# Second cross-attention stream of a decoder layer: VectorE takes all maxima of a unit before its copies and scalings

## The reference, cut to what matters

```python
q = (query @ Wq.T + bq)   # 16 heads of 32; k and v from the context
QEr = jnp.einsum('bhsd,ld->bhsl', q, Er)
Srel = _skew(QEr)
QK = jnp.einsum('bhsd,bhtd->bhst', q, k)
attn = (QK + Srel) / math.sqrt(dh)
attn = jnp.where(causal[None, None], attn, -jnp.inf)
attn = jax.nn.softmax(attn, axis=-1)
out = jnp.einsum('bhst,bhtd->bhsd', attn, v)
x = _layernorm(x + out)
```

## Time and profile before

| | |
|---|---|
| median of 3 runs | 4609.83 us (4608.87 to 4615.19) |
| the profiled execution | 4609.45 us, of which 4607.6 us are the span |
| PE busy | 3910.4 us (85%) |
| DVE busy | 2465.7 us (54%) |
| ACT busy | 1573.2 us (34%) |
| POOL busy | 902.6 us (20%) |
| maxima L785 | 512 instructions, 373.3 us |
| transposes L1127 | 2304 matmuls, 321.9 us |
| mean granted TensorE clock | 0.952 |

### The profile page before, as it was taken

The page is one execution under the profiler, slowest core; times in us unless marked ns, Lnnn a source line. Parts: engine busy times, 40 slices in busy tenths (PEclk is TensorE's granted clock), DMA queues, the critical chain, the costliest instruction groups (busy, mean ns, idle before and its releaser), DMA issues. The chain is left out here.

```text
span 4607.6 us, 89417 instructions
## 1 busy us (share of the span) xinstructions
PE 3910.4 (85%) x36730; PEld 2369.2 (51%) x36730; DVE 2465.7 (54%) x4665; ACT 1573.2 (34%) x3005; POOL 902.6 (20%) x1012
## 2 busy tenths in 40 slices
PE   6999897889998878799988787999887837999992
PEld 3666444546664445466644454666444523444441
DVE  3666335766664357666643576767335763222224
ACT  2444125744441257344412573444125710000000
POOL 2333100113331001133310011333100101222220
PEclk8999899999999999999999999999999978999996
DMA  7332258633322586332225863322258613544545
GB/s 245 102 88 83 83 194 305 202 102 102 90 82 83 198 303 202 104 102 86 82 83 205 299 203 107 95 86 81 83 205 301 205 67 91 125 114 125 127 116 167
DMA packets 257093, 659.34 MB, mean 143 GB/s; under 512 B 20752, under 2 KB 70080, under 8 KB 253456
## 3 DMA queue, kind: packets, MB, share of 16 engines
q1 hardware_dynamic: 241264, 616.06, 40.2%
q0 software_dynamic: 15120, 35.46, 4.0%
q10 hardware_dynamic: 320, 2.23, 0.1%
HBM read 384.84 MB, written 210.11 MB: 129 GB/s over the span
## 5 line engine op out<-in xcount | busy, mean ns | idle before, releaser
L481 ACT ACTIVATE sc<-sc,nmax 128x1024 f32<-128x1024 f32 x512 | 587.3, 1147 | 904.0 <-DVE nmax L679 903.2
L445 POOL TENSOR_SCALAR sc<-sc,pinv 128x1024 f32<-128x1024 f32 x512 | 572.5, 1118 | 1357.3 <-DVE pinv L687 1340.5
L951 PE MATMUL psum<-pts,wct 32*64 32x256 f32 x8192 | 470.3, 380 | 69.8 <-PEq L946 64.5
L679 DVE CUSTOM_DVE_ANT_0 sc<-psum,table_a 128x1024 f32<-128x1024 f32 x256 | 313.2, 1224 | 346.7 <-PE psum L935 252.4
L951 PE MATMUL psum<-xall,wct 32*64 32x256 f32 x8192 | 473.4, 380 | 19.2 <-issue 19.1
L785 DVE CUSTOM_DVE_ANT_0 sc<-psum,big 128x896 f32<-128x896 f32 (+7 forms) x512 | 373.3, 748 | 216.2 <-PE psum L1113 177.7
L925 PE MATMUL psum<-xt,w_all 128*128 128x256 f32 x1792 | 419.2, 387 | 15.0 <-PEq L920 15.0
L481 ACT ACTIVATE sc<-sc,xmax 128x896 f32<-128x896 f32 (+7 forms) x512 | 394.5, 772 | 70.1 <-DVE xmax L785 64.7
L951 PEld LDWEIGHTS psum<-pts,wct 32*64 32x64 f32 x8192 | 331.5, 133 | 157.3 <-issue 121.3
L925 PEld LDWEIGHTS psum<-xt,w_all 128*128 128x128 f32 x1792 | 333.0, 191 | 141.1 <-issue 99.9
L455 POOL TENSOR_SCALAR_AFFINE_SELECT big<-big 128x256 f32<-128x256 f32 (+1 forms) x192 | 92.6, 482 | 1325.2 <-DMA big<-skew_d 1325.1
(11 more groups left out here) (160 smaller groups left out, 5634.1 us busy)
## 6 DMA issues: line engine op xcount, KB each, us to landing
wct<-xall SPq DMA_DIRECT2D x576, 128.0 KB, 2.4
big<-skew_d SPq DMA_DIRECT2D x48, 1024.0 KB, 5.2
w_sb<-w_dram SPq DMA_DIRECT2D x48, 1024.0 KB, 5.4
big<-skew_d SPq DMA_DIRECT2D x48, 768.0 KB, 4.4
table_a<-rows_d SPq DMA_DIRECT2D x33, 960.0 KB, 5.6
table_b<-rows_d SPq DMA_DIRECT2D x33, 960.0 KB, 7.7
big<-skew_d SPq DMA_DIRECT2D x32, 896.0 KB, 4.6
big<-skew_d SPq DMA_DIRECT2D x32, 640.0 KB, 4.7
```

Of the source, the lines that this page charges most:

```text
L445: pool.tensor_scalar(sc[k % 4][:, :], sc[k % 4][:, :], pinv[:, k % 4:k % 4 + 1], 1.0, ALU.mult, ALU.mult).then_inc(probs_scaled, 1)
L481: act.activation(tile, tile, ACT.Exp, bias=least, scale=-1.0, accum_out=total).then_inc(probs_ready, 1)
L679: dve.tensor_tensor_reduce(sc[k % 4][:, :], SLOT[h], table[h][:, off:off + S], -1.0, BIG, ALU.add, ALU.min, nmax[:, k % 4:k % 4 + 1]).then ...
L951: mm = pe.matmul(OSUM[HEAD[h], a, :], v_all[rows, ST * (b % GROUPS) + b // GROUPS, HEAD[h]], ptf[h][rows, QG * b:QG * b + QG], start=(b == ...
```

## The change

On VectorE, in the loop of the second stream, the maxima of all heads of unit u are taken before the two parts. The parts keep the copies, the reciprocal and the scaling, in the order they had. No other engine's code is changed, and no wait, buffer or instruction is added or removed.

```diff
@@ -821,11 +821,10 @@
                     for t in range(ST):
                         if LAST[XV - ST + t] + 7 == u:
                             row_stats(t)
+                    if u < NU:
+                        for i in range(len(UNITS[u][2])):
+                            add_relative(u, i)
                     for part in range(2):
-                        if u < NU:
-                            nh = len(UNITS[u][2]) // 2
-                            for i in range(nh * part, nh * part + nh):
-                                add_relative(u, i)
                         if 1 <= u < NU + 1:
                             half = -(-TURNS[u - 1] // 2)
                             for g in (range(half), range(half, TURNS[u - 1]))[part]:
```

## The result

Over 20 runs of each the changed kernel takes 4600.25 us (median, 4590.91 to 4611.43) against 4613.45 us before (4604.31 to 4627.61). The ratio is 0.9973, with a 95% interval from 0.9965 to 0.9981: 12.5 us, 0.27% faster. The forecast was 4591.5 us, 18 us faster, with a range from 4576 to 4608. In the profiled execution the span is 4599.9 us.

The account below looks back on a forecast made before the run. TensorE's scores waited for VectorE's maxima (134.6 us), its weighing for the scaling (67.8 us). Per batch -2.14 - 3 x 0.85 + 0.2 = -4.5 us, four batches -18: 4591.5 us, range 4576 to 4608.

Parts of the forecast that it names:

- The gain: Iterations making scores of the first halves (two heads) of tiles 5 to 7: next scores 0.88 us sooner each, 2.64 together.
- No gain: Iterations of the second halves of tiles 5 to 7: full or nearly full of TensorE work; only 0.05 us gained, in 5b.
- Iterations 0 and 1: Iterations of tiles 0 and 1: what 0 gives, 1 takes back waiting for the last exponential; nothing for the two.
- The cost: Iterations of tiles 2, 3 and both halves of 4: weighing waits for the scaling, now behind all maxima; 1.84 us lost.
- The sum: A steady quad, twelve iterations: -2.64 - 0.05 + 1.84 = -0.85 us, from 48.07 to 47.2.
- first quad: First twelve units of a batch, starting behind a mask: 2.14 us shorter.
- last quad: Last quad of a batch, row statistics ahead of maxima in 5b to 7a: 0 to 0.6 us lost, 0.2 taken.
- The clock: Rival, iterations 2 to 4a: TensorE idles before weighings and its clock halves; 3 us per steady quad, 4628 us; 11%.
- The exponentials: Rival, 5b, 6b, 7b: transposes wait for ScalarE's second exponential, 0.3 us in hand; 12 us back, 4603 us; 14%.
- The scaling hidden: Rival, iterations 2 to 4b: weighing doesn't stand behind the scaling, so the cost falls away; 45 us faster, 4564; 5%.
- nothing moves: Rival, all iterations: TensorE's own queue sets every one, so gain and cost are gone; 4609 us; 4%.
- The VectorE rule: VectorE's queue, alternative reading: next operation waits until the pipeline empties, so full durations count; quad -1.1 us, 4588 us.

Follow-up runs that it names:

- e1: All maxima first except in iterations 2, 3, 4a and 4b, which keep the old order; against the kernel before: 4569.19 us, ratio 0.9896.
- e2: All maxima first only in iterations 2, 3, 4a and 4b, old order elsewhere; against the kernel before: 4641.4 us, ratio 1.0053.
- e3: Changed kernel with the scaling directly behind all maxima, ahead of the copy, in iterations 2 to 4b: 4560.43 us, ratio to before 0.9877.
- e4: Changed kernel with the scaling between the two halves of the maxima in iterations 2 to 4b, copies behind: 4541.31 us, ratio to before 0.9837.
- e5: Changed kernel with the last group of transposes of iterations 2 and 3 made three times: 4589.1 us, ratio to before 0.9951.
- e8: The kernel of e5 run again, beside a repeat of the changed kernel: 4589.84 us, ratio to before 0.9952.
- e6: Changed kernel with one extra, unused ScalarE copy ahead of its first copy in 5a, 6a and 7a: 4606.06 us, ratio to before 0.9987.
- e7: The changed kernel run again without further change, beside e8: 4597.6 us, ratio to before 0.9972.

## Why the prediction was right, and where it was not

**The gain (5a, 6a, 7a).** Forecast 3.06, 3.34, 3.60; measured 3.09, 3.35, 3.62. The mechanism and the size were right. e1 shows it alone.

**No gain (5b, 6b, 7b).** Forecast 3.76, 4.21, 4.66; measured 3.75, 4.21, 4.66. That these were full of TensorE work was all that the rows had to show.

**Iterations 0 and 1.** This step failed, by a little. Forecast: 1 takes back what 0 gives, 6.11 us for the two. Measured: 2.44 and 3.49, 5.93. In the trace of before the transposes of 1 started as soon as the scores allowed, 0.65 after them, not when the last exponential was there; in the trace after, the last of them waited 0.25 us for it. So the earlier scores helped until the exponential became the later of the two, and 0.18 was gained.

**The cost (2, 3, 4a, 4b).** Forecast 4.23, 5.17, 4.43, 4.65; measured 4.15, 5.12, 4.42, 4.64. The cost is 1.69 instead of 1.84, mostly because a maximum of 384 columns follows the last by 0.48, not 0.49, one of 512 by 0.61 (forecast 0.62), and the weighing of 8 matmuls holds TensorE for 0.36, not 0.38. e2 shows the cost alone, e3 and e4 that it is the scaling in TensorE's way: one copy less in front of it gives 0.6 per iteration, the scaling between the maxima takes the cost away and more.

**The sum.** With the clock at its upper level the quad went from 48.06 to 46.95, -1.11 instead of -0.85. A first quad took 56.6 to 56.9 us before and 54.3 to 54.9 after, -2.2 on average against the -2.14 of the forecast; a last quad without a fall became 1.07 shorter up to its last scores, against 0.65. Four batches of 2.2 + 2 x 1.11 + 1.07 are 22 us, and e5 and e8, in which the clock holds in all steady quads, measure it: ratio 0.995, 22 us.

**The clock.** This was the rival with 11%, and its mechanism is what happened, at the place named, in nearly every steady quad; what was wrong was its price, and so which side of zero it lay on. It was put at 3 us per steady quad, from a whole 4a at half clock and part of iteration 3. A fall lasts only a part of an iteration here (0.69 over 4a), and 4a has some 0.5 us of waiting that it fills: the price is 1.06 to 1.14 where it falls in 4a, 0 to 1 in iteration 3, and 9 us in all. So the forecast of 18 us came out near the measured 12.5 by two errors: 4 us too little gain from the iterations, 9 us too little loss to the clock, which the likeliest case had at nothing. That they partly cancelled is luck. What failed is the evidence "against", which took iteration 2 alone (2.49 busy of 3.86 to 2.42 of 4.16, forecast 2.49 of 4.2) for a change too small to matter. Iteration 3 behind it went from 3.36 of 4.70 to 3.28 of 5.12, and TensorE stood still for 1.74 and 1.84 us before the two weighings, close to the 1.9 forecast. e5 and e8 show that the waits in 2 and 3 together are the cause: filled, they left 24 of 24 steady quads without a fall, against 3 of 24 where they weren't. Which of the two counts more was not tried, and the longest wait alone doesn't tell: before the change TensorE stood still for up to 1.56 us (in 7a) with one fall in 12 quads, and in e1 for at most 0.79 with two. By the Trainium skill (TensorE: Matmul & The Clock Gate, "Why this matters for your kernels") long idle gaps between bursts of matmuls cost the clock. e5 agrees that idle time costs it, with matmuls of no use in the gaps and all steady quads at 1.00; e1 shows that here it needed no long gap.

**The exponentials.** The rival didn't come true, by less than was claimed. The 0.3 us in hand in 5b was 0.14: that step took the head's data as ready at the end of the exponential, and e6's trace puts them later (the exponential ran from 824.08 to 825.01, the read of its row sum from 824.90 to 825.10, and the load goes at 825.15). The 0.3 claimed for 6b was right.

**The scaling hidden, nothing moves.** Both fell: the waits moved by 67 and by 82 us.

**The VectorE rule.** In the changed kernel maxima of 768 columns, 0.96 us long, start 0.88 apart (822.43, 823.31). A copy of 512 columns, 0.69 us long, is followed after 0.60 (824.19, 824.79). The full duration isn't what counts, so the terms by rows were the right ones.

## What to carry to other kernels

When work is moved forward in one engine's queue, list for every iteration which waiting engine it serves and which it keeps standing. Here the same edit gained 2.8 us in eight iterations of a quad and lost 1.7 in the other four, and giving each iteration the order that it needs (e4) was worth six times the change. Here the short step that TensorE waited for (a scaling of 0.2 us) belonged ahead of the long ones, as soon as its input was there.

The waits moved onto TensorE cost twice here: their length, and what the clock took in the same iteration or the one behind. Don't look at the longest idle stretch alone: in the steady quads of the changed kernel none was longer than 1.84 us, and before the change one of 1.56 came back in every quad with hardly a fall.

## What the runs showed of the hardware

The kernel became 8 to 10 us faster by 16 groups of useless transposes per batch, as they kept TensorE's clock at 1.00 in all steady quads: extra work of 0.87 us in the waits of iterations 2 and 3 made no iteration longer. Without them the clock fell in 10 and in 11 of 12 steady quads, mostly in the same iteration of a batch's quads but not in the same from batch to batch (3 in the first batch, 4a in the others in the first trace; 3 in the second batch, 4a in the others in e7's). Where in 3 or 4a it falls decides what it costs, from next to nothing (5.15 us for an iteration 3 at a clock of 0.67, against 5.12) to 1.1 us in 4a; a longer fall in e2 cost 2.7 us (7.10 for 4a at 0.52). What sets this place was not tried.
